# A head in which the first layer's W2 is loaded in 32-wide blocks and turned by VectorE

## What is computed

```python
def ffn(x, W1, W2, W3):                      # W1, W3: 1024 x 256; W2: 256 x 1024
    hidden = silu(x @ W1.T) * (x @ W3.T)
    hidden = fwht(hidden)                    # Walsh-Hadamard transform of 1024 columns
    return hidden @ W2.T

xn = layernorm(x)
x = x + mixer0(xn) * silu(ffn(xn, L0_W1, L0_W2, L0_W3))      # mixer0: matrix products, rmsnorm
xn = layernorm(x)
x = x + attention(xn) * silu(ffn(xn, L1_W1, L1_W2, L1_W3))   # causal, 512 rows
```

## Time and profile before

| | us |
|---|---|
| median of 3 runs | 356.49 (356.45 to 356.65) |
| the profiled execution | 356.77 |
| its span, first to last instruction | 355.0 |
| TensorE busy | 349.0 (98%) |
| VectorE busy | 252.7 |
| ScalarE busy | 167.2 |
| GpSimd busy | 106.1 |

### The profile page before, as it was taken

The page is one execution under the profiler, slowest core; times in us unless marked ns, Lnnn a source line. Parts: engine busy times, 40 slices in busy tenths (PEclk is TensorE's granted clock), DMA queues, the critical chain, the costliest instruction groups (busy, mean ns, idle before and its releaser), DMA issues.

```text
span 355.0 us, 4951 instructions
## 1 busy us (share of the span) xinstructions
PE 349.0 (98%) x1769; PEld 296.2 (83%) x1769; DVE 252.7 (71%) x498; ACT 167.2 (47%) x324; POOL 106.1 (30%) x122
## 2 busy tenths in 40 slices
PE   7999999999999999999999999999999999999996
PEld 4877888888888888888978878888888888888896
DVE  5679964995499666966488876788557886466645
ACT  2865442447244713454465643654346544464510
POOL 2164510366126943663025030150300703004000
PEclk9999999999999999999999999999999999999999
DMA  7989759206160303130341401616014251054001
GB/s 243 250 173 231 151 103 129 83 20 143 37 145 15 120 0 118 34 118 0 118 127 45 129 2 60 185 38 194 4 58 142 69 164 45 3 189 133 3 2 59
DMA packets 69648, 34.44 MB, mean 97 GB/s; under 512 B 40692, under 2 KB 69624, under 8 KB 69624
## 3 DMA queue, kind: packets, MB, share of 16 engines
q1 hardware_dynamic: 69480, 34.06, 38.0%
q10 hardware_dynamic: 144, 0.07, 0.1%
HBM read 21.99 MB, written 12.12 MB: 96 GB/s over the span
## 4 chain that ended last, share of the span: by engine, by line
PE 89%; SPq 4%; DMA 2%; ACT 2%; DVE 2%; issue 1%; ACTq 0%
PE GU L356 19%; PE GU L358 18%; PE GU L357 18%; PE O L356 8%; PE O L357 8%; PE O L358 8%; DMA stage<-in_L_ffn_W 2%; SPq L241 1%; SPq L232 1%; PE O L424 1%; PE T L357 1%; PE T L358 1%; PE T L356 1%; SPq L302 1%; PE O L507 1%; PE O L506 1%
## 5 line engine op out<-in xcount | busy, mean ns | idle before, releaser
L718 ACT ACTIVATE hf<-GU 128x512 f32<-128x512 f32 x64 | 38.2, 599 | 79.9 <-DVE hid L835 63.7
L991 DVE TENSOR_TENSOR hf<-hf,GU 128x512 f32<-128x512 f32 x64 | 43.5, 679 | 28.5 <-PE GU L358 22.6
L356 PE MATMUL GU<-XT,W1T 128*128 128x512 f32 x128 | 50.6, 396 | 0.1
L835 DVE TENSOR_TENSOR hid<-hf,hid 128x512 fp32r<-128x512 f32 x64 | 50.5, 791 | 0.3
L358 PE MATMUL GU<-XT,W1T 128*128 128x512 f32 x128 | 49.9, 390 | 0.0
L357 PE MATMUL GU<-XT,W1T 128*128 128x512 f32 x128 | 49.9, 390 | 0.0
L356 PE MATMUL GU<-XT,W3T 128*128 128x512 f32 x128 | 49.8, 389 | 0.0
L358 PE MATMUL GU<-XT,W3T 128*128 128x512 f32 x128 | 49.8, 389 | 0.0
L357 PE MATMUL GU<-XT,W3T 128*128 128x512 f32 x128 | 49.8, 389 | 0.0
L356 PE MATMUL O<-hid,W2hi 128*128 128x512 f32 x112 | 43.9, 392 | 0.0
L357 PE MATMUL O<-hid,W2hi 128*128 128x512 f32 x112 | 43.7, 390 | 0.0
(11 more groups left out here) (201 smaller groups left out, 717.7 us busy)
## 6 DMA issues: line engine op xcount, KB each, us to landing
swap_rows<-GX SPq DMA_DIRECT2D x7, 512.0 KB, 3.3
sT<-swap_rows SPq DMA_DIRECT2D x28, 128.0 KB, 2.7
swap_gate<-GX SPq DMA_DIRECT2D x7, 512.0 KB, 2.9
sT<-swap_gate SPq DMA_DIRECT2D x28, 128.0 KB, 2.7
stage<-in_L_ffn_W SPq DMA_DIRECT2D x12, 256.0 KB, 4.5
swap_p<-PX SPq DMA_DIRECT2D x4, 640.0 KB, 3.2
PL<-swap_p SPq DMA_DIRECT2D x16, 160.0 KB, 3.2
stage<-in_L_ffn_W SPq DMA_DIRECT2D x32, 64.0 KB, 2.6
```

Of the source, the lines that this page charges most:

```text
L356: pe.matmul(o, lhs(0), rhs(0), start=start, stop=False)
L718: act.activation(hf[:, c % 2, :], GU[:, c % 2, 0, :], ACT.Silu).then_inc(silu_done, 1)
L835: dve.tensor_tensor(dst, src, hi_part.bitcast(F32), ALU.subtract).then_inc(done, 1)
L991: dve.tensor_tensor(hf[:, c % 2, :], hf[:, c % 2, :], GU[:, c % 2, 1, :], ALU.mult).then_inc(mul_done, 1)
```

## The change

- W2 of layer 0 is loaded whole into `U2[0]` by four `load_blocks`, issued behind the first two W1/W3 pairs and hadm. The 16 transposes of W2 on TensorE and the copies of `nat_hi` from PSUM go.
- VectorE turns it in place (`turn_w2(0, j)`, four instructions of 128 x 512), two behind chunk 1 and two behind chunk 2's pair 2. ScalarE copies the hi part (`turned_nat_hi`), and GpSimd, not VectorE, writes the lo part (`nat_lo(0)` to `nat_lo(3)`).
- `stage` is seen as six slots of one W1 or W3 pair half each; only pair 3 waits for a slot (until TensorE has turned pair 0). SyncE's other waits in the head, except those for the exchanges, become one wait for all eight W1/W3 turns.
- x of group 1 is loaded behind pair 2 and the small matrices; win gets a semaphore of its own.
- TensorE's order: x's transposes between the halves of pair 0, three chunks ahead of the first Hadamard product (before: one), the further products behind chunks 3, 4 and 5 (before: 1, 3 and 5).
- ScalarE, VectorE and GpSimd follow that order; GpSimd's list is now: two rstd; residues 0 and 1; pair 0; residue 2; pair 1; rstd of group 1; residue 3; pair 2; quad 0; pair 3; quad 1; last.

```diff
+def first_part(i, w):
+    return first_stage[:, (2 * i + w) % 6, :]
...
-    def load_pair(l, j, to, done):
-        rows = bass.ds(2 * P * j, 2 * P)
-        for w, m in enumerate((W1[l], W3[l])):
-            sp.dma_start(to[:, w, :].rearrange("p (a k) -> p a k", a=2),
-                         m[rows, :].rearrange("(a p) k -> p a k", p=P)).then_inc(done[w], 16)
-        sp.dma_start(to[:, 2, :].rearrange("p (a h) -> p a h", a=2),
-                     W2[l][:, rows].rearrange("(a p) h -> p a h", p=P)).then_inc(done[2], 16)
+    def load_first(i):
+        for w, m in enumerate((W1[0], W3[0])):
+            if i == PAIRS - 1:
+                sp.wait_ge(w_tr, w + 1)
+            sp.dma_start(first_part(i, w).rearrange("p (a k) -> p a k", a=2),
+                         m[bass.ds(2 * P * i, 2 * P), :].rearrange("(a p) k -> p a k", p=P)).then_inc(first_loaded[i][w], 16)
...
-    load_pair(0, 0, stage[:, 0, :, :], stage_loaded[0])
+    load_first(0)
+    load_first(1)
     sp.dma_start(hadm[:, :], consts[:, 1, :]).then_inc(hadm_loaded, 16)
-    load_pair(0, 1, stage[:, 1, :, :], stage_loaded[1])
-    sp.dma_start(X[:, TILES:2 * TILES, :], xt_dram[:, TILES:2 * TILES, :]).then_inc(xnext_loaded, 16)
-    sp.wait_ge(w2_tr, 1)
-    load_pair(0, 2, stage[:, 0, :, :], stage_loaded[0])
+    load_blocks(U2[0][:, :, :].rearrange("p c d -> p (c d)"), W2[0], w2_loaded[0])
+    load_first(2)
     for i, m in enumerate((A_theta, B_real, B_imag, C_real, C_imag)):
         sp.dma_start(ssm[:, i, :, :], m.rearrange("c (a p) s -> p (c a) s", p=P)).then_inc(kv_loaded, 16)
-    sp.dma_start(win[:, :, :], W_in.rearrange("(a p) k -> p a k", p=P)).then_inc(kv_loaded, 16)
+    sp.dma_start(X[:, TILES:2 * TILES, :], xt_dram[:, TILES:2 * TILES, :]).then_inc(xnext_loaded, 16)
+    load_first(3)
+    sp.dma_start(win[:, :, :], W_in.rearrange("(a p) k -> p a k", p=P)).then_inc(win_loaded, 16)
     load_blocks(woutT[:, :, :].rearrange("p m d -> p (m d)"), W_out, wout_loaded)
-    sp.wait_ge(w2_tr, 2)
-    load_pair(0, 3, stage[:, 1, :, :], stage_loaded[1])
...
+    sp.wait_ge(w_tr, 2 * PAIRS)
     load_w(PAIRS)
     move_rows(1)
-    sp.wait_ge(w2_tr, PAIRS)
     load_w(PAIRS + 1)
-    load_blocks(U2[1][:, :, :].rearrange("p c d -> p (c d)"), W2[1], w2_loaded)
+    load_blocks(U2[1][:, :, :].rearrange("p c d -> p (c d)"), W2[1], w2_loaded[1])
     for n in range(1, NB):
...
-    def pair_w2_transposes(i, st, loaded, value):
-        pe.wait_ge(loaded[2], value)
-        src = st[:, 2, :].rearrange("p (a h) -> p a h", a=2)
-        transposes(O[:, 0, :], [src[:, a, c * P:(c + 1) * P] for c in (0, 1) for a in range(KC)]).then_inc(w2_tr, 1)
-    def pair_hadamard(i, nat):
-        pe.wait_ge(w2nat_ready, i + 1)
-        pe.matmul(O[:, 1, :], hadmR[:, :], nat[:, 0, :, :].rearrange("p a d -> p (a d)"), start=True, stop=False)
-        pe.matmul(O[:, 1, :], hadmR[:, :], nat[:, 1, :, :].rearrange("p a d -> p (a d)"), start=False, stop=True).then_inc(h_done, 1)
+    def pair_transposes(i, w, bank):
+        pe.wait_ge(first_loaded[i][w], 16)
+        src = first_part(i, w).rearrange("p (a k) -> p a k", a=2)
+        transposes(bank, [src[:, a, k * P:(k + 1) * P] for k in range(KC) for a in (0, 1)]).then_inc(w_tr, 1)
...
-    def head_pair_w2(i):
-        if i:
-            pe.wait_ge(w2nat_ready, i)
-        pair_w2_transposes(i, stage[:, i % 2, :, :], stage_loaded[i % 2], 16 * (i // 2 + 1))
+        for w in (0, 1):
+            pair_transposes(i, w, T[:, w, :])
...
     def head_hadamard(i):
         if i == 0:
             pe.wait_ge(hadm_ready, 1)
-        if i >= 1:
+        else:
             pe.wait_ge(u_ready, i)
-        pair_hadamard(i, w2nat)
+        pe.wait_ge(natx_ready, i + 1)
+        pe.matmul(O[:, 1, :], hadmR[:, :], w2nat[:, 0, :, :].rearrange("p a d -> p (a d)"), start=True, stop=False)
+        pe.matmul(O[:, 1, :], hadmR[:, :], w2nat[:, 1, :, :].rearrange("p a d -> p (a d)"), start=False, stop=True).then_inc(h_done, 1)
...
-        head_pair(0)
-        first_x_transposes()
-        head_pair_w2(0)
+        pair_transposes(0, 0, GU[:, 0, 0, :])
+        first_x_transposes(0)
+        pair_transposes(0, 1, GU[:, 0, 1, :])
+        first_x_transposes(1)
         head_pair(1)
         first_up_chunk()
+        up_chunk(0, 0, 1, True)
+        up_chunk(0, 0, 2, True)
         head_hadamard(0)
-        head_pair_w2(1)
-        up_chunk(0, 0, 1, True)
+        head_pair(2)
+        up_chunk(0, 0, 3, True)
         head_hadamard(1)
-        head_pair(2)
-        head_pair_w2(2)
-        up_chunk(0, 0, 2, True)
-        up_chunk(0, 0, 3, True)
+        up_chunk(0, 0, 4, True)
         head_hadamard(2)
         head_pair(3)
-        head_pair_w2(3)
-        up_chunk(0, 0, 4, True)
         up_chunk(0, 0, 5, True)
         head_hadamard(3)
         small_natural()
...
     def turned_nat_hi(i):
-        j = i - PAIRS
-        act.wait_ge(h_done, i)
-        hi(w2nat[:, 0, :, :], U2[1][:, 2 * j:2 * j + 2, :], w2_turned, j + 1, natx_hi)
+        l, j = i // PAIRS, i % PAIRS
+        if i:
+            act.wait_ge(h_done, i)
+        hi(w2nat[:, 0, :, :], U2[l][:, 2 * j:2 * j + 2, :], w2_turned[l], j + 1, natx_hi)
...
         chunk(0, 0, True)
         pair_hi(0, 1, 1)
+        chunk(0, 1, True)
+        turned_nat_hi(0)
+        chunk(0, 2, True)
         pair_u(0, 0, 0)
-        nat_hi(1, w2nat)
-        chunk(0, 1, True)
+        turned_nat_hi(1)
+        pair_hi(0, 2, 2)
+        chunk(0, 3, True)
         pair_u(0, 1, 1)
-        pair_hi(0, 2, 2)
-        nat_hi(2, w2nat)
-        chunk(0, 2, True)
-        chunk(0, 3, True)
+        turned_nat_hi(2)
+        chunk(0, 4, True)
         pair_u(0, 2, 2)
         pair_hi(0, 3, 3)
-        nat_hi(3, w2nat)
+        turned_nat_hi(3)
+        act.wait_ge(win_loaded, 16)
         act.wait_ge(kvec_ready, 1)
         for m in range(MC):
             act.activation(win[:, m, :], win[:, m, :], ACT.Identity, scale=kvec[:, m:m + 1]).then_inc(win_scaled, 1)
-        chunk(0, 4, True)
         chunk(0, 5, True)
         pair_u(0, 3, 3)
         hi(gb[:, :, :].rearrange("p g k -> p (g k)"), O[:, 0, 0:2 * KC], gb_tr, 1, gb_ready)
...
+    def turn_w2(l, j):
+        dve.wait_ge(w2_loaded[l], 16 * QUADS)
+        in_place(U2[l][:, 2 * j:2 * j + 2, :].rearrange("p c d -> p (c d)")).then_inc(w2_turned[l], 1)
...
-        nat_lo(0, w2nat)
         chunk(0, 0)
         pair_lo(0, 1, 1)
-        nat_lo(1, w2nat)
         chunk(0, 1)
+        turn_w2(0, 0)
+        turn_w2(0, 1)
+        chunk(0, 2)
         pair_lo(0, 2, 2)
-        nat_lo(2, w2nat)
-        chunk(0, 2)
-        k_vector()
+        turn_w2(0, 2)
+        turn_w2(0, 3)
         chunk(0, 3)
         dve.wait_ge(xnext_loaded, 16)
+        stats(1, TILES)
+        k_vector()
+        chunk(0, 4)
         pair_lo(0, 3, 3)
-        nat_lo(3, w2nat)
-        stats(1, TILES)
-        chunk(0, 4)
         normalise(1, TILES)
         turn_wout()
         chunk(0, 5)
...
     def nat_lo(i):
-        j = i - PAIRS
-        pool.wait_ge(natx_hi, j + 1)
-        pool.tensor_tensor(w2nat[:, 1, :, :], U2[1][:, 2 * j:2 * j + 2, :], w2nat[:, 0, :, :].bitcast(F32), ALU.subtract).then_inc(natx_ready, 1)
+        l, j = i // PAIRS, i % PAIRS
+        pool.wait_ge(natx_hi, i + 1)
...
             pool.tensor_tensor(rstd[:, 2 * h:2 * h + 2], vtmp[:, 2 * h:2 * h + 2], mhalf[:, 2 * h:2 * h + 2], ALU.pow).then_inc(rstd_ready, 1)
+        nat_lo(0)
+        nat_lo(1)
         pair_butterfly(0, 0, 1)
+        nat_lo(2)
         pair_butterfly(0, 1, 2)
+        rstd_of(1)
+        nat_lo(3)
+        pair_butterfly(0, 2, 3)
         quad_butterfly(0, 0, 4)
-        pair_butterfly(0, 2, 3)
-        rstd_of(1)
         pair_butterfly(0, 3, 4)
         quad_butterfly(0, 1, 10)
         last_butterfly(0, 12)
```

More of the change, by code:

```diff
@@ L174, in two_block_kernel @@
         ident_loaded, hadm_loaded, mask_loaded = sem("ident_loaded"), sem("hadm_loaded"), sem("mask_loaded")
+        first_loaded = [[sem(f"first{i}_loaded{w}") for w in (0, 1)] for i in range(PAIRS)]
         stage_loaded = [[sem(f"stage{i}_loaded{w}") for w in range(3)] for i in (0, 1)]
@@ L364, in transposes @@
                 return last
-            def pair_transposes(i, st, loaded, value, bank=T):
-                for w in (0, 1):
-                    pe.wait_ge(loaded[w], value)
-                    src = st[:, w, :].rearrange("p (a k) -> p a k", a=2)
-                    transposes(bank[:, w, :], [src[:, a, k * P:(k + 1) * P] for k in range(KC) for a in (0, 1)]).then_inc(w_tr, 1)
-            def pair_w2_transposes(i, st, loaded, value):
-                pe.wait_ge(loaded[2], value)
-                src = st[:, 2, :].rearrange("p (a h) -> p a h", a=2)
-                transposes(O[:, 0, :], [src[:, a, c * P:(c + 1) * P] for c in (0, 1) for a in range(KC)]).then_inc(w2_tr, 1)
-            def pair_hadamard(i, nat):
-                pe.wait_ge(w2nat_ready, i + 1)
```

(33 more changed lines are left out.)

25 lines of the change are left out of this document (10 added, 15 removed).

## The result

The change makes the kernel slower: 362.14 us median of 5 runs (361.59 to 363.33) against 356.49, a ratio of 1.0157 with a 95% interval of 1.014 to 1.0173. Predicted were 359.4 us, with a range of 357.4 to 361.3. The sign is right, and the size falls short by half: 5.65 us were lost, not 2.9.

What follows compares the result with a forecast made beforehand. TensorE was taken to bound the kernel, so head losses stay. The first down product moves from 47.67 to 50.5, +2.8 (3.0 with roundings kept), taken as 2.9: 356.49 + 2.9 = 359.4 us, range 357.4 to 361.3.

Steps and rivals of the forecast that it cites:

- What bounds the kernel: TensorE, busy 98% of the span: a microsecond won or lost in the head (0 to 48 us) stays so.
- TensorE's order: TensorE's new sequence in the head: new waits eat the 1.45 us to be won, +0.25 us before W2's end.
- The wait for Hadamard 0: TensorE's new wait for the first Hadamard product's operand, until 20.0: 1.7 us, bounds 1.4 and 2.3.
- W2's landing: Layer 0's W2 load in 128-byte pieces at about 143 GB/s lands at some 15.6 us, so it is hidden.
- the 1.4 us to spare: Margin between W2 landing at some 15.6 us and VectorE first asking for it at 17.0.
- GpSimd's chain: GpSimd's residue and butterflies from 30.35, without a gap: last butterfly from 40.6 to 43.0 with collisions.
- The step that failed: VectorE reaches its sums at about 41.2, inside GpSimd's last butterfly, and waits: sums end at 44.1 instead of 41.17.
- The term of 1.6: VectorE's delay ahead of the sums from being held twice by GpSimd, at two hid residues: some 1.6 us.
- the predicted stretch: VectorE's sums, held by GpSimd's last butterfly, stretched to some 2.9 us.
- The chain of 6.17 us behind it: ScalarE and VectorE steps from the sums' end to VR's residue, last release of the first down product: 6.17 us.
- The clock rival: TensorE's granted clock falls to 1.2 GHz for some 5 us behind the second wait: 2.5 us longer, 361.9; chance 0.04.
- the 2.6 us of the prediction: One TensorE wait of 2.6 us ahead of the first down product near 48, put down to VR's residue.

## Why the prediction was right and wrong

- **What bounds the kernel** was right: the head's shift (5.18) is the span's (5.3), and nothing later gives it back.
- **TensorE's order** was right. The wait for Hadamard 0 is 1.68 (1.7 said) and Hadamard 3 waits 0.21. It starts at 32.35, not 31.85: 0.5 us late, of which 0.33 were there at Hadamard 0 (20.33, not 20.0), and 0.22 of these at the first chunk (10.20, not 9.98).
- **W2's landing** was hidden, as said, but the 1.4 us to spare were not there. The sum left out SyncE's issuing: the last of the four parts was issued at 10.8 us, and none took less than 6.2 to land, so it came at 17.0 or later and not at 15.6. With the load four times quicker to issue, 0.4 us come back at most.
- **GpSimd's chain** was right. The last butterfly ran from 40.76 to 43.15; 40.6 to 43.0 was said.
- **The step that failed** is "VectorE comes to the sums at about 41.2 (39.57 before, and some 1.6 from being held twice)". It came at 45.44. The term of 1.6 was mis-sized by 4.2 us: to the shift of 5.87 the normalise gives 2.85, which the sum put at nothing, the later start of it all 1.1, also put at nothing, and the two residues 1.9, for which alone the 1.6 stood. Since the sums so came behind the last butterfly and not into it, 1.7 us of the predicted stretch (2.9 for 1.18) were saved, and 2.5 remained: sums' end 46.6, not 44.1. The chain of 6.17 us behind it was right to the hundredth (5.49 to the start of its last step, in both).
- **Why it was mis-sized.** I took the hold to apply to VectorE instructions with two SBUF inputs, because the rows that I had (chunk residues, sums) are of that form, and so left the normalise at its 1.38. Of the Trainium skill's rule I had quoted one half. "SBUF — State Buffer" (SBUF: two separate sides) names an operation in a mode that uses both ports beside one with two inputs, and "VectorE: DVE Perf Modes" (What auto-detection actually checks) lets a single-source operation from SBUF to SBUF take such a mode. By these the normalise is held; the traces agree, 4.23 us for 1.38. The 1.6 for the two residues came near (1.9), in part by luck: its row of such a hold has 0.7 us more than usual, and here they took 0.68 and 1.23 more than before. A VectorE instruction waits for what is left of the GpSimd instruction that it meets, up to 1.8 us behind the last butterfly. The late start was in the change itself, which moves pair 3's residues behind chunk 4; the sum followed VectorE only from the sums on.
- **The clock rival** (0.04) was a real mechanism. It didn't fall here, where the longest wait is 1.7 us, but it fell in some runs of the kernels with a wait of 2.0 us. Had the 2.6 us of the prediction come in one piece, 0.04 would have been too low.

That the normalise's hold is a term of this size is shown: taking it away gave 2.7 us of the head back and 2.4 of the time at full clock (359.7), and adding work beside it in the kernel before cost 2.8. That the terms add is not: the residues alone also give 3.0 back, since each removal also decides what meets what next. Why the runs of after spread over 1.7 us (361.59 to 363.33) with the clock at 0.999 or more in all was not tried.

## What to carry to other kernels

Before moving work to GpSimd, list every VectorE instruction of that stretch with its operands in SBUF, the one-input ones like tensor_scalar too (look in a trace which kinds are held: transposes and statistics were not), and charge each with the rest of the GpSimd instruction that it will meet; then draw the order again with these delays in it, for a shift of 1 us can move a short instruction into the longest one. A VectorE step moved late must be followed through the queue that ships its result, with all the issuing behind it. Where the new order leaves TensorE one wait of 2 us, two levels of time are possible (three of the seven kernels with such a wait in their profile kept the full clock in it); weigh a few idle matmuls against them.
